# The last 254 nodes as two groups of one column, and the x part of the first layer one group ahead, in a one-core graph-network kernel

## The reference

```python
h = jnp.maximum(_layernorm(x, axis=-1), 0.0)             # x: 12500 x 128
agg = jax.ops.segment_sum(edge_attr, dst, num_segments=12500)   # 200000 x 128, dst sorted
h = jnp.concatenate([h, agg], axis=-1)
h = jax.nn.relu(h @ W1 + b1)                             # W1: 256 x 128
h = jax.nn.relu(h @ W2 + b2)
h = h @ W3 + b3
out = x + layernorm(h) * ln_w + ln_b                     # float32 throughout
```

## Time and profile before

| engine | busy us | share of the span |
|---|---|---|
| PE | 280.1 | 90% |
| DVE | 233.1 | 75% |
| PEld | 182.3 | 58% |
| ACT | 156.8 | 50% |
| POOL | 134.0 | 43% |

### The profile page before, as it was taken

How to read it: one execution, slowest core, us unless ns; L and a number is a source line. 1 busy time by engine, 2 the same in 40 slices (tenths; PEclk the granted TensorE clock), 3 DMA queues, 4 the chain that set the end, 5 groups by cost and what they waited for, 6 DMA issues and landing times.

```text
span 312.4 us, 12913 instructions
## 1 busy us (share of the span) xinstructions
PE 280.1 (90%) x3955; PEld 182.3 (58%) x3955; DVE 233.1 (75%) x879; ACT 156.8 (50%) x413; POOL 134.0 (43%) x203
## 2 busy tenths in 40 slices
PE   2959999999999999999999999999999999999992
PEld 0746666656666666666556656565556565655671
DVE  4954777788787778777788777777787777777754
ACT  1442445555555545455555544545545545455533
POOL 7735334444444344444444443334444433444510
PEclk9976999999999999999999999999999999999998
DMA  7999999999999999999999999999999999999996
GB/s 237 342 377 373 373 373 372 372 376 383 383 383 383 383 383 384 383 383 384 383 383 383 383 383 382 384 384 383 382 383 383 383 383 383 384 382 384 384 392 217
DMA packets 83284, 116.50 MB, mean 373 GB/s; under 512 B 7116, under 2 KB 83272, under 8 KB 83272
## 3 DMA queue, kind: packets, MB, share of 16 engines
q1 hardware_dynamic: 82368, 116.06, 103.9%
q10 hardware_dynamic: 904, 0.28, 0.4%
HBM read 109.92 MB, written 6.40 MB: 372 GB/s over the span
## 4 chain that ended last, share of the span: by engine, by line
SPq 36%; PE 28%; issue 13%; DVE 11%; ACT 5%; DMA 4%; ACTq 1%; DVEq 1%
SPq L344 19%; SPq L379 13%; PE part_ps L497 10%; PE place_ps L508 7%; DVE onehot L973 4%; PE hid_ps L531 4%; ACT h L736 4%; PE hid_ps L541 3%; DMA ring<-in_edge_attr 3%; SPq L339 2%; DVE agg L1065 1%; DMA dst_i<-in_dst 1%; DVE x_mv L954 1%; DVE x_shift L966 1%; SPq L388 1%
## 5 line engine op out<-in xcount | busy, mean ns | idle before, releaser
L899 POOL TENSOR_SCALAR place<-iota,rows_at 128x128 f32<-128x128 f32 x130 | 84.4, 650 | 136.3 <-PE place_ps L508 127.8
L497 PE MATMUL part_ps<-ring,onehot 128*32 128x128 f32 x3120 | 113.7, 280 | 7.5 <-DMA ring<-in_edge_attr 3.2
L497 PEld LDWEIGHTS part_ps<-ring,onehot 128*32 128x32 f32 x3120 | 78.6, 110 | 66.1 <-issue 40.1
L1065 DVE TENSOR_TENSOR agg<-place_ps,agg 128x128 f32 x130 | 37.8, 291 | 58.6 <-PE place_ps L508 56.4
L508 PE MATMUL place_ps<-place,part 128*128 128x128 f32 x260 | 64.0, 329 | 2.9 <-ACT part L722 2.9
L973 DVE TENSOR_TENSOR onehot<-iota,local_t 128x768 f32<-128x768 f32 x65 | 62.4, 961 | 0.1
L736 ACT ACTIVATE h<-xs,x_shift,x_rstd 128x128 f32 (+2 forms) x98 | 41.3, 483 | 32.8 <-DVE x_shift L966 32.6
L508 PEld LDWEIGHTS place_ps<-place,part 128*128 128x128 f32 x260 | 39.5, 191 | 30.0 <-issue 21.5
L722 ACT ACTIVATE part<-part_ps 128x128 f32<-128x128 f32 x130 | 34.6, 267 | 25.3 <-PE part_ps L497 25.3
L907 POOL TENSOR_TENSOR xs<-xs,vecs 128x384 f32 (+2 forms) x33 | 33.6, 1019 | 27.0 <-ACT h L736 27.0
L531 PE MATMUL hid_ps<-agg,w1a 128*128 (+2 forms) x64 | 28.8, 532 | 7.3 <-DVE agg L1065 7.3
(11 more groups left out here) (103 smaller groups left out, 203.9 us busy)
## 6 DMA issues: line engine op xcount, KB each, us to landing
ring<-in_edge_attr SPq DMA_DIRECT2D x260, 384.0 KB, 8.2
xs<-in_x SPq DMA_DIRECT2D x32, 192.0 KB, 7.6
out_x<-xs SPq DMA_DIRECT2D x8, 384.0 KB
out_x<-xs SPq DMA_DIRECT2D x104, 24.0 KB
dst_i<-in_dst SPq DMA_DIRECT2D x1, 768.0 KB
out_x<-xs SPq DMA_DIRECT2D x2, 192.0 KB
tail_e<-in_edge_attr SPq DMA_DIRECT2D x1, 192.0 KB, 5.1
out_x<-xs SPq DMA_DIRECT2D x1, 168.0 KB
```

What stands on the lines that cost most here:

```text
L497: last = nc.tensor.matmul(part_ps[par_q % 2][s * WIN:(s + 1) * WIN, 0:D], onehot[:, oct_par, first + s, j, :], e[:, s, j * D:(j + 1) * D], ...
L899: nc.gpsimd.tensor_scalar(place[:, par_q % 2, :], iota[:, 0:P], rows_at[:, k:k + 1], None, ALU.is_equal).then_inc(place_ready, 1)
L1065: nc.vector.tensor_tensor(v, place_ps[par_q % 2][:, 0:P], v, ALU.add).then_inc(added, 1)
```

## The change

The last 254 nodes become two groups of one column each: `FORE`, 126 nodes from node 12246, and `AFT`, the last 128 nodes. FORE needs the sums up to quad 128 only (`QUADS - 1` adds), AFT those up to quad 129. Each is taken through layers 1 to 3 by itself, with 128 columns: FORE in bank `ht_ps`, AFT in `hid_ps`, their third layers in `part_ps[0]` and `part_ps[1]`. The bias product is gone; DVE adds the bias for both as it does elsewhere. Statistics, normalisation and transposes of the two are still done together at the start (`LAST`, now 128 rows x 2).

Group 31's x rows are loaded, normalised, transposed and multiplied before group 0, in a bank of its own, `top_ps`, which holds the result until the end. To have that bank, layers 1 and 2 of all other groups share `hid_ps`. In the loop, statistics, transposes and x part in step i are all those of group i+1; ACT's loop holds one step where it held two.

```diff
-LAST_PARTS = ((0, LAST_CUT), (LAST_CUT, LAST_P))
+FORE, AFT = GROUPS, GROUPS + 1
+AFT0 = NODES - P
+FORE_N = AFT0 - LAST0
+FORE_PARTS = ((0, FORE_CUT), (FORE_CUT, FORE_N))
...
-        ht_ps, hid1_ps, hid2_ps, y_ps = bank("ht_ps"), bank("hid1_ps"), bank("hid2_ps"), bank("y_ps")
+        ht_ps, hid_ps, top_ps, y_ps = bank("ht_ps"), bank("hid_ps"), bank("top_ps"), bank("y_ps")
...
                 load_quad(0, 0)
-                for p0, p1 in LAST_PARTS:
-                    sp.dma_start(xg(LAST)[p0:p1, :], last_rows(x, p0, p1)).then_inc(last_x_loaded, 16)
+                for g in (FORE, AFT):
+                    sp.dma_start(xs[:, last_column(g)], last_rows(x, g, 0, P)).then_inc(last_x_loaded, 16)
+                sp.dma_start(xg(TOP), group_rows(x, TOP)).then_inc(top_x_loaded, 16)
                 load_x(0, 0, 0)
-                load_x(1, 1, 0)
...
-                    store_last(GROUPS + 1, LAST_PARTS[:1])
+                    store_last(FORE, FORE_PARTS[:1])
+                    store_last(AFT, ((0, P),))
...
                         if q == 1:
+                            transpose_h(TOP)
+                        elif q == 3:
+                            layer1_x(TOP)
+                        elif q == 4:
                             transpose_h(0)
-                    transpose_h(1)
-                    layer1_x(0, 0)
+                    layer1_x(0)
...
-                                layer1_x(i + 1, 1 - par)
+                                transpose_h(i + 1)
                             else:
-                                transpose_h(i + 2)
+                                layer1_x(i + 1)
...
-                    def step(i, par):
+                    def step(i):
                         q = 4 * i + AHEAD
                         relu1(i)
                         copy_part(q, AHEAD)
                         relu2(i)
+                        x_sqrt(i + 1)
                         copy_part(q + 1, AHEAD + 1)
-                        x_sqrt(i + 2)
-                        normalise(i + 2)
+                        normalise(i + 1)
                         copy_part(q + 2, AHEAD + 2)
+                        copy_ht(i + 1)
                         y_sqrt(i)
                         copy_part(q + 3, AHEAD + 3)
-                        copy_ht(i + 2, par)
...
-                    relu2(g + 1)
-                    relu1(LAST)
-                    relu2(LAST)
-                    square_y(g + 1)
-                    power_sqrt(g + 1)
-                    square_y(LAST)
-                    act.wait_ge(y_rstd_done, g + 2)
-                    power_sqrt(LAST)
+                    relu2(TOP)
+                    relu1(FORE)
+                    relu1(AFT)
+                    relu2(FORE)
+                    relu2(AFT)
+                    square_y(TOP)
+                    power_sqrt_top()
+                    square_y(FORE)
+                    square_y(AFT)
+                    power_sqrt_last()
...
-                        stats_x(i + 2, x_loaded[par], 16 * pairs + 32)
+                        stats_x(i + 1, x_loaded[1 - par], 16 * pairs + 16 * (1 + par))
+                        mean_x(i + 1)
                         add(q + 1, 0, base[1])
-                        mean_x(i + 2)
+                        scale_x(i + 1)
+                        shift_x(i + 1)
                         make_onehot(2 * i + 5, 1)
-                        scale_x(i + 2)
-                        shift_x(i + 2)
...
-                    take_y(g + 1)
-                    weigh_y(g + 1)
-                    weigh_y(LAST)
-                    scale_y(g + 1)
-                    output(g + 1)
-                    scale_y(LAST)
-                    output(LAST)
+                    take_y(TOP)
+                    weigh_y(TOP)
+                    take_y(FORE)
+                    take_y(AFT)
+                    weigh_y(FORE)
+                    weigh_y(AFT)
+                    scale_y(TOP)
+                    output(TOP)
+                    scale_y_last()
+                    output_last(FORE)
+                    output_last(AFT)
```

More of the change, by code:

```diff
@@ L1264, in group @@
                         finish(g)
[L1266 to L1268 removed]
+                    with dve.Fori(0, TOP // 2) as t:
                         group(2 * t, 0, t)
@@ L1271, in general @@
                     group(TOP - 1, 0, TOP // 2)
-                    group(TOP, 1, TOP // 2)
-                    finish(LAST)
+                    finish(TOP)
+                    for g in (FORE, AFT):
+                        take_y(g)
+                        weigh_y(g)
+                    scale_y_last()
+                    output_last(FORE)
+                    output_last(AFT)
                 branch(dve, fast, general)
```

325 lines of the change are left out of this document (169 added, 156 removed).

## The result

The changed kernel takes 315.36 us (median of 22 runs, 314.93 to 317.36); the kernel before took 314.66 in the runs beside them. The ratio is 1.003, 95% interval 1.0019 to 1.004: slower by about 0.9 us (0.6 to 1.3). The profiled execution took 315.37 with a span of 313.5, where that of before took 314.22 with 312.4. The median of before over these runs is 0.44 above its profiled execution, so part of the 1.1 between the two spans is not the change's.

A forecast was written before the change was run, and what follows sets the result against it. The DMA queue was taken as the bound, 8.98 us a step against 8.55 for compute. Terms -0.36 + 0.1 = -0.26 took 314.22 to 313.96, plus 0.16 for the median: 314.1 us; forecast 313.7 to 314.6, outer range 313.3 to 315.4.

The forecast's parts named there:

- dear packets: Rival, x loads at the start: 129 more packets of 512 B cost 1.4 us, time 315.4; chance 0.05.
- The loop: Steps of the loop: stay at about 8.55 us, bounded by 8.0 and 9.1, under the transfers' 8.98; no cost.
- The cover: Loop: a ready step of 8.55 us against 8.98 for transfers; 0.4 us of slack a step hides delays.
- The loop becomes the bound: Rival, loop: new chain 0.7 longer, step 9.25; 30 steps cost 8.1 us, some 4 absorbed, time 318; chance 0.08.
- The end, PE: PE's order after the last quad's sums: layer 2 of TOP 0.79 us earlier, layer 3 0.78, PE done 0.9 earlier.
- The end, ACT and DVE: After the last relus: ACT's squares and the outputs 0.46 us earlier; DVE's added operations fit beside the squares, 0.1 cover left.
- The last store: Three stores on SP at the end: last issue 0.36 us earlier, at 308.75 instead of 309.11; what follows unchanged, 3.3.
- The start: Loads before the loop: 129 more packets, through 512 B x rows, cost 0.1 us; PE's later start hidden by the queue.
- The sum: Whole kernel: -0.36 for the last store plus 0.1 for the start gives -0.26 us.

The follow-up runs named there:

- the run that measured them: Kernel before, its last 254 x rows loaded by column as 512 B packets, in four transfers of 112 and 15 rows: 315.02 us, ratio 1.001.

## Why the prediction was wrong

It said 314.1 us, no change that can be measured, or a gain of 0.26 us. A loss of 0.9 came, 315.36. Of the distance, 0.3 is that before has a median of 314.66 over more runs, not 314.38. The time still lies inside the outer range of 313.3 to 315.4, but by luck: that upper bound was put there for dear packets, which did not come.

**The loop is the step that failed.** "The same work per step" was true, and the order was read rightly. From the step's sums part, h is done after 6.08 us (6.12 was said), the transposes start at +6.13, the fourth placement at +7.40 (+7.47 was said). So the loop got a term of 0, its step staying under the transfers. What I did not ask was which operations of different engines now lie on top of each other. From the step's start h is done 1.2 earlier (6.08, before 7.27), and POOL's addition, which waits for h, starts 0.8 earlier (6.63, before 7.45), onto a product that moved by only 0.17 (6.87, before 7.04). The text said that the sums part waits for the add as before; instead the add, and the copy behind ACT's root, waited for that product. I took durations from rows of before as properties of the instruction, when one of them, 0.54, held only in that company. The row of POOL at 82.38, 0.41 behind the product's start, was there to be read.

**The cover was the wrong measure.** I set the step against 8.98 and called the 0.4 us between them hidden. For the queue that is right, 8.60 is under it. But the last step has no step behind it in which to catch up. There the chain product, mean, root, copy, placement, sums part counts in full: 0.71 us, of which 0.54 goes with POOL's addition. The sums part that it ends in came 1.2 later, TOP's 1.15 later, 0.35 of it perhaps the edges'. That the last quad would start within 0.3 of 301, as my text asked, failed with 302.38.

**The rival "The loop becomes the bound"** had the place and not the mechanism: a ready step stayed under 8.98 and the queue stayed full (DMA share 1.04 to 1.07 from 15 us to 307). A threshold between 8.60 and 9.21 there is: with 9.21 the loss was 12 us, where by my 8.1 less 4 I had given a step of 9.25 only 4. I had left out that the loop's slack was in use, to make good the late start.

**The end, PE.** Layer 2 of TOP starts 0.79 behind quad 129's sums, as predicted. Its layer 3 is 2.36 behind where 2.2 was said and 3.02 was before. But 0.22 of the gain had been paid ahead: the placement of 128 now stands between TOP's sums part and 129's sums, which start 1.00 apart and not 0.78. The text counted from 129's sums and took their start as given.

**The end, ACT and DVE.** 0.46 was said, 0.25 came. The squares start at +4.65 where +4.39 was said: AFT's sums part comes 0.13 late, and a relu of 128 columns from PSUM takes 0.37 us, not the 0.28 that I had from a copy:

```profile
304.94 0.37 ACT L794 ACTIVATE h_t<-ht_ps,b1s 128x128 f32<-128x128 f32 x1 [0.34 <-PE ht_ps L584]
...
305.82 0.37 ACT L794 ACTIVATE h_t<-hid_ps,b1s 128x128 f32<-128x128 f32 x1 [0.52 <-PE hid_ps L584]
```

DVE's added operations fitted beside ACT's squares, as said: the two products run from 307.99 to 308.47, ACT's root ends at 308.34, and TOP's output starts at 308.60.

**The last store.** I let AFT's issue start 0.15 behind its rows. It started at about 310.46, 8.08 behind quad 129's sums, where 8.10 was before and 7.75 was said. The next issue on SP came 0.5 us behind the one before, not 0.34. What follows the last issue took 3.04 instead of 3.29, which gave most of it back; why is not settled.

**The start.** 0.1 was said, the 512 B rows measure 0.3 with 0.45 either way, so the term stands. The rate of 13 to 15 us did fall:

```profile
13.00:15.00 2.00, 2.00 (x25) 1.06 (x27) 1.90 (x5) 1.12 (x3) 0.33 (x1) 1.00 0.77 236
```

Before it was 312 GB/s. But from 0 to 15 us both moved nearly the same (282 and 285 GB/s), so this isn't where 0.9 us went. The rival of dear packets falls with the run that measured them: 1.4 us lies outside its interval. That run has the loads alone; the stores of 512 B, which the sum left out (83557 packets in all, 273 more than before), are in the kernel with the new end and the old loop, whose interval ends at 0.6 us.

**The sum again,** in the terms of the prediction: the outputs -0.08 for -0.46 (-0.25 behind quad 129's sums, +0.17 ahead of them), the third store +0.23 for +0.10, the loop's last step +0.71 for 0. The first two leave the new end with next to nothing, which the kernel with the new end and the old loop bears out (1.0008). The rest of the span's 1.1 is 0.49 by which the last quad of the loop starts later, 0.35 of it the landing, and -0.25 behind the last issue; neither is told apart from chance.

## What to carry to other kernels

When an edit moves an operation in time, read which instructions of the other engines it will now overlap, above all POOL and DVE on two SBUF operands each, and price the pair, not the parts. Slack in a transfer-bound loop covers every step but the last: draw the chain from the last loop step to the end by itself. Of two contending operations, let the one on the chain issue first: exchanging two lines brought the product from 1166 ns to 583. Count an end from a point that the edit doesn't move: from quad 129's sums the new end gains 0.25 us, from TOP's sums part 0.03.

## What was not expected of the hardware

- DVE's product of 128 x 384 with both operands in SBUF takes 0.52 to 0.63 us alone or first, and 1.13 to 1.37 when it is held by POOL's addition of the same size, which started 0.05 to 0.29 ahead; it then ends 0.40 to 0.42 behind POOL's end. POOL's takes 0.99 to 1.02 when it is first and 1.00 to 1.10 when it starts 0.31 to 0.43 behind DVE's, ending 0.85 to 0.88 behind it. Twice in 30 steps of one kernel POOL's row starts 0.05 or 0.06 ahead and POOL is the one held, for 1.44 and 1.45 us.
- Two transfers of 127 rows took SP 4.0 us to issue and held the next two for 3.9, with the DMA share down to 0.07; in 112 and 15 rows an issue is 0.46 us.
- A store's issue costs the same for 14 rows as for 128 (two issues on SP take 0.86 us with 112 and 14 rows, 0.84 with 112 and 128): a third store is a third issue.
